# A two-layer graph network on one Trainium2 core: the column one-hot rows of the logit sums move from VectorE to GpSimd

## The reference

```python
feat = concatenate([n_f[edge_src], n_f[edge_dst]], axis=1)
e_hh = relu(feat[:E_HH] @ W_hh + b_hh)          # 256 edges
e_oo = relu(feat[E_HH:E_HH + E_OO] @ W_oo + b_oo)   # 1280 edges
e_ho = relu(feat[E_HH + E_OO:] @ W_ho + b_ho)   # 6656 edges
logit = (concatenate([e_hh, e_oo, e_ho]) @ W_a + b_a)[:, 0]
alpha = softmax of logit over the edges of each destination
z_f = segment_sum(alpha[:, None] * n_f[edge_src], edge_dst)
h_new, o_new = relu([n_f, z_f][:128] @ W_hn + b_hn), relu([n_f, z_f][128:] @ W_on + b_on)
```

## Time and profile before

| | |
|---|---|
| time, median of 3 runs | 657.75 us (657.56 to 659.94) |
| time of the profiled execution | 657.6 us |
| its span in the profile | 655.6 us |
| TensorE products, busy | 561.7 us (86%) |
| TensorE weight loads | 415.1 us (63%) |
| VectorE | 477.3 us (73%) |
| ScalarE | 287.5 us (44%) |
| GpSimd | 176.7 us (27%) |
| moved by DMA | 140.5 MB, 214 GB/s over the span |

### The profile page before, as it was taken

One profiled execution on the slowest core, in us unless ns is written; L12 is line 12 of the kernel. 1 busy time (PEld: TensorE's weight loads), 2 busy tenths in 40 slices (PEclk: granted clock), 3 DMA queues, 4 the chain that ended last, 5 costly groups with the idle time before them and its releaser, 6 DMA issues.

```text
span 655.6 us, 8151 instructions
## 1 busy us (share of the span) xinstructions
PE 561.7 (86%) x2373; PEld 415.1 (63%) x2377; DVE 477.3 (73%) x934; ACT 287.5 (44%) x466; POOL 176.7 (27%) x164
## 2 busy tenths in 40 slices
PE   0799999999859996979898997567949999869987
PEld 0688777776626774656575764333738878657866
DVE  6715266776998999989989996486796289783252
ACT  2622321113076555556655465489852183322200
POOL 2000200265464754565536553300030000000000
PEclk9999999999879998989898998788978899969999
DMA  8444553499999999999999998853456066121021
GB/s 315 140 137 151 184 189 109 149 277 382 304 299 349 308 317 303 349 314 337 299 350 304 289 349 285 191 178 113 130 178 239 16 227 196 60 82 47 0 81 48
DMA packets 55973, 140.51 MB, mean 214 GB/s; under 512 B 6274, under 2 KB 6402, under 8 KB 55938
## 3 DMA queue, kind: packets, MB, share of 16 engines
q0 software_dynamic: 20624, 74.98, 37.6%
q1 hardware_dynamic: 27072, 50.34, 22.7%
q10 hardware_dynamic: 8242, 14.75, 6.0%
HBM read 123.27 MB, written 16.78 MB: 214 GB/s over the span
## 4 chain that ended last, share of the span: by engine, by line
PE 40%; DVE 30%; DMA 15%; issue 7%; ACT 4%; POOL 3%; ACTq 0%; DVEq 0%; POOLq 0%
PE ps L615 22%; DMA gath<-tab_b,tabl_i 10%; DVE gath L870 6%; PE ps L601 6%; DVE ring_l L845 4%; DVE gath L865 4%; PE ps L774 3%; DMA tab_b<-stage 3%; DVE onehot L887 2%; PE ps L746 2%; PE ps L565 2%; ACT onehot L474 2%; PE ps L759 2%; DMA gath<-tab_a,tabl_i 2%; POOL gath L287 2%
## 5 line engine op out<-in xcount | busy, mean ns | idle before, releaser
L615 PE MATMUL ps<-ring_h,actT_h 128*128 128x512 f32 x520 | 228.2, 439 | 25.7 <-ACT stage L445 9.1
L615 PE MATMUL ps<-ring_h,actT_l 128*128 128x512 f32 x520 | 208.6, 401 | 0.0
L615 PE MATMUL ps<-ring_l,actT_h 128*128 128x512 f32 x520 | 207.7, 400 | 0.0
L474 ACT ACTIVATE onehot<-onehot,lgs 128x512 bf16<-128x512 bf16 x192 | 124.6, 711 | 96.3 <-DVE onehot L887 87.8
L427 ACT CAST ring_h<-raw 128x512 fp32r<-128x512 f32 x176 | 104.8, 617 | 117.5 <-PE ps L615 86.3
L845 DVE TENSOR_TENSOR ring_l<-raw,ring_h 128x512 fp32r<-128x512 f32 x176 | 116.8, 685 | 31.9 <-ACT ring_h L427 31.4
L615 PEld LDWEIGHTS ps<-ring_h,actT_h 128*128 128x128 f32 x520 | 101.0, 194 | 60.5 <-ACT stage L445 12.0
L615 PEld LDWEIGHTS ps<-ring_h,actT_l 128*128 128x128 f32 x520 | 100.6, 194 | 23.0
L287 POOL DMA_INDIRECT gath<-tab_a,tabl_i x64 | 73.0, 1141 | 156.3 <-DVE gath L870 71.7
L615 PEld LDWEIGHTS ps<-ring_l,actT_h 128*128 128x128 f32 x520 | 101.4, 195 | 20.7
L565 PE MATMUL ps<-onehot 128*128 128x512 bf16 x290 | 83.9, 398 | 23.7 <-ACT onehot L474 19.7
(11 more groups left out here) (157 smaller groups left out, 488.9 us busy)
## 6 DMA issues: line engine op xcount, KB each, us to landing
raw<-in_L_gnn_W_ho_dram SPq DMA_DIRECT2D x32, 256.0 KB
raw<-in_L_gnn_W_oo_dram SPq DMA_DIRECT2D x32, 256.0 KB
raw<-in_L_gnn_W_hh_dram SPq DMA_DIRECT2D x32, 256.0 KB
raw<-in_L_gnn_W_on_dram SPq DMA_DIRECT2D x32, 256.0 KB
raw<-in_L_gnn_W_hn_dram SPq DMA_DIRECT2D x32, 256.0 KB
tab_a<-stage ACTq DMA_DIRECT2D x24, 256.0 KB
tab_b<-stage ACTq DMA_DIRECT2D x24, 256.0 KB
raw<-in_L_gnn_W_dram SPq DMA_DIRECT2D x16, 256.0 KB
```

Source lines behind the costliest of these rows:

```text
L474: ins = nc.scalar.mul(onehot[:, s, 1 + i, :], onehot[:, s, 1, :], lgs[:, i, q:q + 1])
L615: mm = nc.tensor.matmul(ps[:, first + m, :], w, v, start=(k == 0 and i == 0), stop=(k == KT - 1 and i == 2))
```

## The change

For the logit sums, VectorE writes only the row one-hot (part 1). The column one-hot (part 0) is written by GpSimd with the same operation. In GpSimd's loop over the tiles, column_onehot(q - 13) stands behind the gathers that belong to tile q; the thirteen that are left stand behind the last gather. Each waits on s_ohu for its slot and counts up a new semaphore, s_ohc, for which TensorE waits ahead of each tile's sum. The schedules SUM_AT, SLOT and SLOT_FREE are only moved up in the text. The one-hots of the earlier edge counts (L796, L797) stay with VectorE.

```diff
+        s_ohc = sem("column_onehots_ready")
...
+            def column_onehot(q):
+
+                pool.wait_ge(s_ohu, SLOT_FREE[q])
+                nc.gpsimd.tensor_scalar(onehot[:, SLOT[q], 0, :], iota_f[:, :], node_f[:, q, 0:1], None, ALU.is_equal).then_inc(s_ohc, 1)
+
             LAG = 2
+            BEHIND = 13
             FIRST = 5
...
                 if q - LAG >= FIRST and q - LAG not in PLAIN:
                     gather_add(q - LAG, kinds_of(q - LAG))
+                if q >= BEHIND:
+                    column_onehot(q - BEHIND)
             for q in range(ET - LAG, ET):
                 gather_add(q, 3)
+            for q in range(ET - BEHIND, ET):
+                column_onehot(q)
...
             def add_logits(q, place, s):
 
+                pe.wait_ge(s_ohc, q + 1)
                 pe.wait_ge(s_part, q + 1)
                 accumulate(reg[0], place, s, 3)
...
                 dve.wait_ge(s_ohu, SLOT_FREE[q])
-                for j, e in ((0, 0), (1, 2)):
-                    ins = nc.vector.tensor_scalar(onehot[:, SLOT[q], j, :], iota_f[:, :], node_f[:, q, e:e + 1], None, ALU.is_equal)
-                ins.then_inc(s_oh, 1)
+                nc.vector.tensor_scalar(onehot[:, SLOT[q], 1, :], iota_f[:, :], node_f[:, q, 2:3], None, ALU.is_equal).then_inc(s_oh, 1)
```

More of the change, by code:

```diff
@@ L217, in gnn_kernel @@
         TP_Z = TP_ATT + KT
+        FIRST_COUNTS = 2
+        LAST_COUNTS = FIRST_COUNTS + ET // (2 * KT) - 1
+        SUM_AT = {(6 + i, k): i * TC + k for i in range(6) for k in range(TC)}
+        SUM_AT |= {(12, k): 42 + k for k in range(8)}
+        SUM_AT |= {(13, k): 50 + k for k in range(2)}
+        SUM_AT |= {(13, 4 + k): 52 + k for k in range(4)}
+        SUM_AT |= {(14, k): 56 + k for k in range(6)}
+        SUM_AT |= {(15, k): 62 + k for k in range(2)}
+        assert sorted(SUM_AT.values()) == list(range(ET))
+        SLOT, SLOT_FREE, user = {}, {}, {s: ET - OS + s for s in range(OS)}
+        for (_, k), q in sorted(SUM_AT.items()):
+            SLOT[q] = k % OS
+            SLOT_FREE[q] = OS + user[k % OS] + 1
+            user[k % OS] = ET + q
         @block.sync
@@ L361, in bank_done @@
                 chunk_done(eng, q)
[L364 to L374, removed]
         EARLIER = 12
@@ L383, in gnn_kernel @@
             SPLIT_AT[(c - 1, KT - 1) if c < 15 else (14, 4)] = (min(tiles), max(tiles) + 1)
[L385 to L389, removed]
         LAST_OF_KIND = (T_HO - 1, T_HO + T_OO - 1, ET - 1)
```

## The result

| | before | after |
|---|---|---|
| time, median | 658.60 us (4 runs, 657.56 to 659.94) | 672.23 us (4 runs, 670.86 to 675.64) |
| ratio | | 1.0214 [1.0169, 1.0258] |
| profiled execution, its span | 657.6 us, 655.6 us | 672.37 us, 670.6 us |
| VectorE busy | 477.3 us | 482.2 us |
| GpSimd busy | 176.7 us | 297.5 us |

The changed kernel is 2.1% slower, 13.6 us by the medians. The number forecast, 672.3, is met almost to the digit. The working behind it is not. The experiments show that VectorE's gain, 11.9 us in the sum, was worth 3.9, and that the price, 24.9 in the sum, was 18.6 and was paid in another way. The two errors nearly cancel, and GpSimd's queue paces most of the stage where the sum had VectorE's.

A forecast was written before the change was run, and what follows sets the result against it. The prediction took VectorE's queue to pace the gather stage, the gather loop close behind. Sum: 657.6 - 11.9 (VectorE's one-hots) + 24.9 (holding by GpSimd) + 1.7 (the end) = 672.3 us, range 652 to 690.

The forecast's parts named there:

- the third rival: Gather stage: VectorE wins every contest and GpSimd's queue decides at 5.25 us a tile, +32 us, 692 us; chance 0.17.
- the forecast (0.42): Gather stage: the engines hold one another and VectorE paces; 672.3 us, from 663 to 682; chance 0.42.
- VectorE loses 11.9 us: VectorE's queue in the gather stage: 45 one-hots fewer at 0.265 us each, taken off the time in full.
- the second rival: Gather stage: no holding, but the gather loop takes VectorE's gain back; 659.3 us, no change; chance 0.18.
- The GpSimd one-hot, 0.88 us: Length of one 128x512 one-hot on GpSimd, the middle between 0.61 and 1.16 us, built from a cast and memsets.
- GpSimd's own queue, 4.37 us a tile, just fits: GpSimd in the gather stage: 3.19 us of gathers plus 0.88 + 0.30, within the 4.53 us a tile lasts.
- The hold, 24.9 us: Gather stage: GpSimd one-hots keep VectorE standing during its one-hots and two-input operations, 0.55 us a tile, 45 tiles.
- the 63%: Share of the 204 us stage, 128.3 us, in which VectorE runs one-hots or two-input operations and would be held.
- the sum's own rule: Time before, less VectorE's 11.9 us, plus 0.63 of the GpSimd one-hot's length for 45 tiles, plus 1.7 us.
- Waits for slots, 17 of up to 5 us: GpSimd in the loop: 17 of 51 one-hots would wait for a freed slot, at most some 5 us; costed at nothing.
- The end, +1.7 us: Last sums on TensorE: sum 49 late but covered, tile 51's one-hot ready at 424.8 against 423.03; 1.7 us, 0 to 3.
- The marks that were named: Profile signs: longer two-input operations (L845, L865, L870), stage some 13 us longer, VectorE almost without waits, sum 49 late.

The follow-up runs named there:

- the memsets: Changed kernel with each GpSimd column one-hot replaced by three write-only memsets of the same tile, each waited for; 664.35 us, ratio 1.0115, run beside the changed kernel.
- 32 columns: Changed kernel with GpSimd writing only the first 32 of 512 columns of each column one-hot, all waits kept; 658.27 us, ratio 0.9984.
- 224 columns: Changed kernel with GpSimd writing only the first 224 of 512 columns of each column one-hot; 662.22 us, ratio 1.0035.
- the tail alone: Changed kernel with GpSimd writing column one-hots of tiles 49 to 63 only, VectorE both for the others; 661.21 us, ratio 1.0019.

## Why the prediction was right, and where it was not

**The direction and the place** were right: slower, in the stage of the gathers, with the two engines holding one another. The mechanism was right in part only: what the stage shows is the third rival, GpSimd as the bound (chance 0.17), under the time of the forecast (0.42). That the time was met to the digit is luck.

**VectorE loses 11.9 us.** The busy time was sound (0.253 us each by the kernel with no column one-hots, 0.265 in the sum). What it is worth was not: 3.9 us of time. The step that failed is the sentence that VectorE's queue sets the pace, with the loop close behind. It is in series with the loop: of 11.3 us taken off it in the stage, 7.7 came back as waits for gathers. That was the second rival, and it took eight of the twelve.

**The GpSimd one-hot, 0.88 us.** It takes 1.56 alone and 2.05 in place. Both bounds, 0.61 and 1.16, were too low. The step that failed is the bound itself: the earlier trace rows hold a cast and memsets, and a comparison with a scalar is another kind of operation, 2.5 times a cast of its size. The text allowed for a dearer one only as the third rival made worse, and that is what came. The figure that the text had from the GPSIMD Engine Reference of the Trainium skill (section 3.1), 769 ns for 512 elements as the best case of a tight loop, is off in the same direction: 1563 ns were measured.

**GpSimd's own queue, 4.37 us a tile, just fits.** It is 4.99 a tile. With 2.05 in place of 0.88 the prediction's own row gives 3.19 + 0.30 + 2.05 = 5.54, above what was measured, since the record of an issue partly overlaps the next one (the one-hot of 211.65 begins 0.55 us before the record of the gather ahead of it ends). Against the 4.53 that a tile lasted it does not fit, and the verdict turns: the third rival, GpSimd as the bound, is what the groups of the stage show. Its price was 32 us in the stage; 21.5 were measured, because its 5.25 us a tile were a little too long.

**The hold, 24.9 us.** It exists, and with the access that was named: the memsets show two-input operations held only when GpSimd reads. Its size and its owner were mis-sized. VectorE is busy 482.2 us against 461.1 without any column one-hot: 21.1 / 64 = 0.33 us a one-hot, where the sum had 0.55 for a much shorter one. Some 8 us of it lie on the edge rows and adds with two inputs (by the groups over the span, L882 84.4 against 78.4 and L877 39.1 against 37.5), most of the rest on one-hots and small ones with a single input, which the memsets stretch as well. L857, 34 of the 128 us on which the 63% rested, is hardly held: 688 ns against 683. The larger share falls on GpSimd, 2.05 - 1.56 = 0.49 us a one-hot, which the sum did not count at all; the third rival had it, as 0.6. This share does not grow with the length: mean against shortest, 32 columns take 0.88 and 0.36 us, 224 columns 1.32 and 0.84, 512 columns 2.03 and 1.56, about half a microsecond more each time. VectorE's share does: 0.03, 0.13 and 0.33 us a one-hot, by its busy time. In time the reading is worth 8.8 us, by the two kernels run side by side, with the looseness said there.

SBUF — State Buffer, of the Trainium skill (section "Who interferes with whom"), has it that whichever starts first keeps the other out for its whole instruction. The pairing that it names is borne out (edge rows at 1320 ns over the span with reading, 1228 without). The whole-instruction part is not: during the 2.55 us of the one-hot at 202.52 VectorE was in L877 or L882 nearly throughout, and yet the one-hot lost only 0.96 us and L882 0.38, so that the two ran beside one another for about a microsecond.

**Why the number came out.** With the length that was measured, 1.56, the sum's own rule gives 657.6 - 11.9 + 45 x 0.63 x 1.56 + 1.7 = 691.6. With the length it assumed, the kernel takes 1.0035 of the time before (the 224 columns). A length too short by almost half and a price per microsecond that was too high cancelled, by luck. By the experiments the changed kernel's 14.7 us are made of: VectorE's gain, -3.9; a full GpSimd queue that only writes, +9.8 (664.35 - 654.57); the reading, +8.8 (673.14 - 664.35). The last two make the 18.6 us that stand against the sum's 24.9; their sum is firmer than the split between them. The middle term still holds what writing does to VectorE's single-input operations; the runs don't part it.

**Waits for slots, 17 of up to 5 us.** In the stage they came to 0.7 us. They were laid out for a queue that keeps its pace; a queue that is late finds its slots free. In the kernel with 32 columns, whose queue is not late, they do come: 8 waits, 12.8 us, the longest 4.0.

**The end, +1.7 us.** By itself right: with the tail alone sum 49 began at 413.31 and sum 51 at 424.77, forecast 413.0 and 424.8. In part that is luck, too: the one-hot of tile 49 took 2.22 us instead of 0.88, but the gather of tile 62 was issued 0.74 us earlier than in the kernel before, and the one-hot's record overlaps that of the issue ahead of it. In the full change it is lost in something that the prediction did not follow. In the kernel before GpSimd stood ahead of the gather of tile 62 until the last tables had landed (in the chain that ended last, the store of tab_b stands shortly ahead of it: start us, us, what; then the gather):

```profile
393.16 13.37 DMA tab_b<-stage
...
408.40 1.53 POOL L287 DMA_INDIRECT gath<-tab_a,tabl_i  x1 [9.95 <-issue]
```

In the changed kernel, some 20 us later in the work, hardly any of that wait is left:

```profile
421.70 1.00 POOL L305 DMA_INDIRECT gath<-tab_a,tabl_i  x1 [0.72 <-issue]
```

So a stage that ends later absorbs a wait behind it, and the end is shorter by 5.4 us, although sums 49 and 51 now wait 6.7 us for column one-hots. That is why the stage's 21.5 us show as 15 in the span. With 27 tiles on GpSimd the same wait takes up nearly the whole 7.1 us of the stage: the part from sum 48 to the last sum falls from 61.6 to 55.4 us.

**The marks that were named.** Two of the three means did rise, that of L845 by only 5 ns, and sum 49 was late: right in the main. The stage grew by 21.5 us where 13 were named, and VectorE waited 22.9 us for gathers where it was to stand almost without waits: by the text's own mark that says that the loop, or GpSimd, paces. It does.

## What to carry to other kernels

Before work is moved to an engine that stands in a loop with the one relieved, add up that engine's queue per turn with the durations of the very operation, and set it against the turn: here 2.7 us of issues, 2.05 of one-hot and the gaps between them, against a turn of 4.5. Where the trace has no row of that operation, a row of another kind of the same size is no upper bound. And ask first what the removal alone can bring (here 3.9 us of 16 busy): where two engines wait for one another, what is taken off one can come back as its wait for the other. And read the stage beside the time: a wait behind the stage can hide what the stage has lost.

## What the runs showed of the hardware

- On GpSimd an operation with a scalar on 128x512 took 1.49 to 1.56 us and a copy or cast of the same tile 0.61; the type of the input (half or bfloat16) and the operation (comparison or multiplication) made no such difference.
- Exclusion between VectorE's operations with two inputs and GpSimd's reading is not even-handed: back to back, six of VectorE's kept a one-hot waiting for all their 3.69 us and lost nothing; of the 44 edge rows in the stage 13 lost about 0.4 us (1.59 to 1.69 us against 1.22). On average GpSimd loses half a microsecond an operation, whether it has 32 columns or 512. Why L857 is nearly never held is open.
- Writing alone holds VectorE's one-hots (423 ns on average with memsets, 350 without), but not its operations with two inputs (1228 and 1207 ns).
- The granted clock of TensorE in the stage fell from 0.96 to 0.91, a mean of stretches at 2.4 and at 1.2 GHz, while TensorE's share of busy time there fell from 93% to 86%. Whether that costs anything of its own was not tried.
